# Sixteen units of attention and feed-forward on one core: the first unit's attention starts one unit earlier, and three smaller edits

## The chip, the cores and the metric

One core of one Trainium2 chip runs the whole program. The metric is the device time in microseconds (us). The kernel before takes 980.73 us, the median of three runs (980.03 to 981.28).

## The reference, cut to what matters

```python
x = x + _layernorm(attn(_layernorm(x)))      # x: 4 x 1024 x 512, float32
x = x + _layernorm(ffn(_layernorm(x)))

def attn(x):                                 # 16 heads of 32, chunks of 128 rows
    q, k, v = split(x @ w_qkv.T + b_qkv)     # 512 -> 3 * 512
    # per chunk and head, with S carried from chunk to chunk
    inter  = einsum(q * decay_q, S)
    scores = einsum(q, k) * dmask
    out    = inter + einsum(scores, v)
    S      = lam_c * S + einsum(k * decay_k, v)
    return out @ w_out.T + b_out

def ffn(x):                                  # weights rounded to float8_e4m3fn, then used as float32
    return ((silu(x @ gate_w * gate_s) * (x @ up_w * up_s)) @ down_w) * down_s   # 512 -> 1536 -> 512
```

## The kernel before, in words

The 4096 rows are 16 units of 256 rows (two tiles of 128). Float32 numbers are carried as a float16 half and a float16 rest (hi and lo), so one product is two or three float16 matmuls. The program is written as five queues by hand, one for each engine: TensorE (PE) multiplies, ScalarE (ACT) makes the hi halves and the normalised rows, GpSimd (POOL) makes the lo halves, the roots of the variances and the residual sums, VectorE (DVE) empties PSUM, and SyncE (SP) issues nearly all DMAs. Every engine runs its queue strictly in order, and semaphores hold it where it needs another one.

There are four stages. **Preparation** loads the QKV weights in four pieces (`w_in`), takes their largest value (DVE L1280, one reduction for each piece), spreads it over the partitions with a matmul (`spread_w_max`), makes a power of two of it, and splits the weights into hi (ACT L490, `w_hi`) and lo (DVE L1304, `w_lo`), for k, v and q in this order. ACT turns to `x_normalise(1)` and `x_hi(1)` between the second and the third `w_hi`. Unit 0's q doesn't wait for the split: `project_first` computes it from the float32 weights, output by output, once all four pieces are there. **Ahead**: for k = 0 to 13 (`LEAD` is 14) `ahead(k)` projects q, k and v of unit k and spills them to DRAM; DVE also rounds the feed-forward weights there. **Mixed slots**: `first_slot` runs the attention of unit 0 between the projections of unit 14, `second_slot` runs the attention of unit 1, the output projection of unit 0 and the projection of unit 15. **Slots** 2 to 17: slot s runs the attention of unit s, the output projection of unit s-1 and the feed-forward of unit s-2.

The steps by their names: `project_qk(n, i)` is 24 matmuls of 256 columns, i = 0, 1 for q and 2, 3 for k; `project_v(n, t)` is 12 matmuls of 512 columns; `scores(s, c, half)` is 8 small matmuls for chunk c, in two groups of heads, into the banks `b_s`; `masked` (DVE L1430) takes them out of PSUM, `probs_hi` (ACT L569) and `probs_lo` (POOL L1118) split them, and `attend(s, c)` multiplies them with v when all four groups of the chunk are split. `carry_and_state(s, c)` is the recurrent part; its sum is split by `state_hi` (ACT L581) and `state_lo` (DVE L1460), and the next chunk's carry waits for it. `k_lo(n, i)` (DVE L1409, L1416) empties a bank of k, and `project_v(n, t)` waits for it where v uses the same banks. `project(u, t)` is the output projection; behind it come `y_moments` (DVE), `inverse_std_of` (POOL L1050, L1053, L1057), `y_normalise` (ACT), `residual` (POOL L1128), `x1_moments`, again a root, `x1_hi` (ACT), `x1_lo` (POOL L1132) and a transposing DMA (`turn_x1`), and then `gate_up(u, 0)` (PE L919).

A bank is shared between stages: units below 14 put v into `b_s`, so that `scores(0, 0, 0)` waits for `v_sum` of unit 13. In the **last slot** only the feed-forward of unit 15 is left: `gate_up` six times, `down` for tile 0 and tile 1 (PE L937), and for each tile the scale (DVE L1532), the moments, the root on POOL, `y2_normalise` on ACT (L493), the sum with x (POOL L1142, `final`) and the store by SP (L400).

## Time and profile before

| | us |
|---|---|
| median of three runs | 980.73 |
| the profiled execution, its own time | 980.54 |
| its span, first to last instruction | 978.7 |
| TensorE busy | 949.6 |
| VectorE, GpSimd, ScalarE busy | 696.8, 691.3, 510.6 |
| granted TensorE clock, mean | 0.997 |

Times in the profile are counted from the start of the span; between the span and the run's own time lie 1.84 us. A line name such as L919 is the line of the source. A row of the timeline has the start, the length, the engine and line, what is written and read, how many instructions are merged, and in brackets how long the engine sat idle before and what released it. Matmuls overlap, so that a row's length is a little more than the distance to the next.

### The profile page before, as it was taken

The page shows a single profiled execution, that of the slowest core. Times are in us where ns is not written, and L with a number is a line of the kernel's source. Part 1 is how long each engine was busy: PE and PEld are TensorE (multiplying, and loading weights), DVE is VectorE, ACT ScalarE, POOL GpSimd, SP SyncE. Part 2 cuts the span into 40 slices and gives each one's busy share as a digit, 9 for nine tenths or more (in the row PEclk, how much of TensorE's full clock was granted, in tenths as well). Part 3 has the DMA queues.
Part 4 walks back from the last instruction along what each step waited for, and adds up shares of the span by engine and source line. Part 5 has one row for each costly group of instructions (what it writes and reads, how often), then busy time and mean ns, then how long its engine had stood idle before and what let it go on. Part 6 is the DMA issues. An engine that isn't in the chain of part 4 may idle for free.

```text
span 978.7 us, 21882 instructions
## 1 busy us (share of the span) xinstructions
PE 949.6 (97%) x8412; PEld 700.8 (72%) x8412; DVE 696.8 (71%) x1357; ACT 510.6 (52%) x987; POOL 691.3 (71%) x839
## 2 busy tenths in 40 slices
PE   8999999999888999999999999999999999999996
PEld 7687777777666776867778776767767676776764
DVE  6999998985887775767567576766757676675422
ACT  5666555565655464636355463635546363544522
POOL 3799998887776585948567584856758495775633
PEclk9999999999999999999999999999999999999998
DMA  9798899989976673846658284665838475512100
GB/s 320 232 309 245 244 261 314 281 260 301 244 204 144 138 195 66 183 108 142 157 103 190 55 199 97 152 146 115 180 59 199 94 161 121 139 44 44 44 23 22
DMA packets 199354, 159.87 MB, mean 163 GB/s; under 512 B 141649, under 2 KB 141777, under 8 KB 199121
## 3 DMA queue, kind: packets, MB, share of 16 engines
q1 hardware_dynamic: 198384, 157.86, 65.3%
q8 instruction: 66, 1.08, 0.5%
q10 hardware_dynamic: 864, 0.61, 0.2%
q14 instruction: 40, 0.32, 0.1%
HBM read 82.93 MB, written 41.94 MB: 128 GB/s over the span
## 4 chain that ended last, share of the span: by engine, by line
PE 44%; DVE 18%; POOL 16%; issue 10%; DMA 4%; SPq 3%; ACT 3%; POOLq 0%; DVEq 0%; ACTq 0%
PE bank L919 18%; PE bank L937 17%; PE att L896 5%; DVE stats L1386 3%; POOL rstd L1053 3%; POOL att_pool L1118 3%; DMA dram_qk<-qk_hl 2%; POOL vv L1103 2%; DVE state_hl L1460 2%; POOL qk_hl L1083 2%; SPq L297 2%; DVE w_pool L1523 2%; POOL xr L1128 1%; POOL rstd L1050 1%; DVE state L1449 1%
## 5 line engine op out<-in xcount | busy, mean ns | idle before, releaser
L919 PE MATMUL bank<-f_pool,up_q 128*128 128x256 f16 x1536 | 183.7, 273 | 4.2 <-DVE w_pool L1523 2.8
L919 PE MATMUL bank<-f_pool,gate_q 128*128 128x256 f16 x1536 | 183.6, 273 | 4.1 <-ACT w_pool L617 3.9
L937 PE MATMUL bank<-down_q,w_pool 128*128 128x512 f16 x768 | 168.3, 379 | 0.0
L919 PEld LDWEIGHTS bank<-f_pool,up_q 128*128 128x128 f16 x1536 | 148.1, 98 | 26.8 <-DVE w_pool L1523 8.5
L919 PEld LDWEIGHTS bank<-f_pool,gate_q 128*128 128x128 f16 x1536 | 146.3, 98 | 26.9 <-ACT w_pool L617 6.5
L1118 POOL TENSOR_TENSOR att_pool<-p,att_pool 128x512 f16<-128x512 f32 x128 | 145.7, 1159 | 24.5 <-ACT att_pool L569 24.5
L1523 DVE SCALAR_TENSOR_TENSOR w_pool<-bank,us_t,w_pool 128x256 f32<-128x256 f32 x192 | 84.1, 480 | 109.9 <-ACT w_pool L617 54.7
L1050 POOL TENSOR_TENSOR rstd<-mv,eps_t 128x1 f32<-128x1 f32 (+1 forms) x113 | 32.4, 287 | 182.0 <-DVE mv L1392 181.8
L937 PEld LDWEIGHTS bank<-down_q,w_pool 128*128 128x128 f16 x768 | 74.1, 98 | 86.9
L1136 POOL TENSOR_TENSOR w_pool<-w_pool 128x512 f16<-128x512 f32 x96 | 111.2, 1164 | 29.3 <-ACT w_pool L623 29.2
L569 ACT CAST att_pool<-p 128x512 f16<-128x512 f32 x128 | 75.6, 619 | 53.7 <-DVE p L1430 53.0
L493 ACT ACTIVATE w_pool<-w_pool,rstd 128x512 f32<-128x512 f32 x32 | 26.0, 812 | 146.1 <-POOL rstd L1057 146.1
L1430 DVE TENSOR_TENSOR p<-bank,mask 128x512 f32<-128x512 f32 x128 | 83.2, 682 | 8.0 <-POOL att_pool L1118 5.3
L617 ACT ACTIVATE w_pool<-bank,gs_t 128x256 f32<-128x256 f32 x192 | 80.1, 467 | 11.8 <-PE bank L919 10.2
L896 PE MATMUL att<-wout_hl,o_t 128*128 128x512 f16 x360 | 80.1, 379 | 0.0
L623 ACT CAST w_pool<-w_pool 128x512 f16<-128x512 f32 x96 | 59.2, 617 | 37.1 <-DVE w_pool L1523 35.9
L1053 POOL TENSOR_TENSOR rstd<-rstd,eps_t 128x1 f32<-128x1 f32 (+1 forms) x113 | 70.7, 626 | 8.8
L1532 DVE TENSOR_TENSOR w_pool<-bank,ds_t 128x512 f32<-128x512 f32 x32 | 22.1, 692 | 76.2 <-PE bank L937 76.2
L896 PEld LDWEIGHTS att<-wout_hl,o_t 128*128 128x128 f16 x360 | 35.2, 98 | 39.3
L1449 DVE TENSOR_TENSOR state<-bank,state_d 32x128 f32<-32x128 f32 x112 | 32.0, 286 | 30.4 <-issue 29.3
L1142 POOL TENSOR_TENSOR w_pool<-xr,w_pool 128x512 f32<-128x512 f32 x32 | 40.7, 1271 | 17.7 <-ACT w_pool L493 17.7
L1460 DVE SCALAR_TENSOR_TENSOR state_hl<-state,state_hl 32x128 f16<-32x128 f32 x112 | 48.1, 430 | 6.0 <-ACT state_hl L581 4.9
(147 smaller groups left out, 1824.4 us busy)
## 6 DMA issues: line engine op xcount, KB each, us to landing
dram_qk<-qk_hl SPq DMA_DIRECT2D x64, 256.0 KB, 4.6
att_pool<-dram_qk SPq DMA_DIRECT2D x64, 256.0 KB, 6.0
f_pool<-dram_qk SPq DMA_DIRECT2D x64, 256.0 KB, 6.0
xr<-in_x SPq DMA_DIRECT2D x31, 512.0 KB, 4.6
dram_kd<-kd_hl SPq DMA_DIRECT2D x32, 256.0 KB, 2.8
dram_v<-vv SPq DMA_DIRECT2D x32, 256.0 KB, 4.4
qn_pool<-dram_qk SPq DMA_DIRECT2D x32, 256.0 KB, 9.1
out_x<-w_pool SPq DMA_DIRECT2D x32, 256.0 KB, 2.1
```

The lines of the kernel that those rows point to most:

```text
L569: nc.scalar.copy(pr_hl[:, 0, heads(g)], by_head(p32[:, g % 2])).then_inc(p_hi_d, 1)
L617: ins = nc.scalar.activation(sil[:, j], b_gate[:, j * TOK:(j + 1) * TOK], ACT.Silu, scale=gs_t[:, 2 * i + j:2 * i + j + 1])
L623: nc.scalar.copy(h_hl[:, 0, 2 * i:2 * i + 2].rearrange("p k t -> p (k t)"), h32[:, i % 2]).then_inc(h_hi_d, 1)
L896: ins = nc.tensor.matmul(b_y[t], o_mov(u)[:, a, k, t * P:(t + 1) * P], wout_hl[:, b, k], start=(k == 0 and n == 0), stop=(k == KT - 1 and ...
L919: ins = nc.tensor.matmul(b[:, j * TOK:(j + 1) * TOK], w[:, k, o * P:(o + 1) * P], x1_hl[:, v % 2, part, k], start=(k == 0 and part == 0), ...
L937: ins = nc.tensor.matmul((b_gate, b_up)[t][:, :], h_hl[:, part, k, t * P:(t + 1) * P], down_q[:, k], start=(k == 0 and part == 0), stop=(k ...
L1053: nc.gpsimd.tensor_tensor(rstd[:, ln, 0, cols], rstd[:, ln, 2, cols], eps_t[:, 1, cols], ALU.pow).then_inc(pow_d[ln], 1)
L1118: nc.gpsimd.tensor_tensor(pr_hl[:, 1, heads(g)], by_head(p32[:, g % 2]), pr_hl[:, 0, heads(g)], ALU.subtract).then_inc(p_lo_d, 1)
L1136: nc.gpsimd.tensor_tensor(h_hl[:, 1, 2 * i:2 * i + 2].rearrange("p k t -> p (k t)"), h32[:, i % 2], h_hl[:, 0, 2 * i:2 * i + 2].rearrange( ...
L1430: nc.vector.tensor_tensor(by_head(p32[:, g % 2]), by_head(b_s[g % 2][:, :]), mask[:, heads(g)], ALU.mult).then_inc(p_d, 1)
L1460: ins = nc.vector.scalar_tensor_tensor(out=state_hl[r, 1, :, r], in0=state[r], scalar=2.0 ** -STATE_SHIFT, in1=state_hl[r, 0, :, r], op0=A ...
L1523: ins = nc.vector.scalar_tensor_tensor(out=h32[:, i % 2, j * TOK:(j + 1) * TOK], in0=b_up[:, j * TOK:(j + 1) * TOK], scalar=us_t[:, 2 * i ...
```

## The change

There are four edits.

1. The attention of unit 0 begins in `ahead(13)`, which is now `last_ahead`: `scores(0, 0, 0)`, `scores(0, 0, 1)` and `carry_and_state(0, 0)` lie between the projections of unit 13. For this v of unit 13 goes to `b_gate` and `b_up` instead of `b_s`. The steps of the first and second slot move up by half a slot on all five queues, and `scores(1, 0, 0)` closes the first slot. In slot 2, PE does `carry_and_state(2, 0)` behind `gate_up(0, 0)` instead of before it.
2. Unit 0's q is computed by weight piece: `project_first(k)` runs the four outputs for piece k as soon as that piece has landed, into four banks. The spreading matmul stands in the middle of piece 2. On DVE, `moments_x(1)` moves from before the largest value's steps to behind them, and so stands directly before the first `w_lo`.
3. In the last slot ACT does `y2_normalise(14, 0)` behind the first silu of unit 15 instead of before it.
4. The last tile is computed in two halves of 256 columns. DVE subtracts the mean itself and multiplies and adds by halves when POOL has the root, and ACT and SP each store one half.

```diff
+            spill_v(LEAD - 1)
             load_xr(0)
-            spill_v(LEAD - 1)
             spill_q(LEAD)
+            turn_o_tile(0, 0)
             sp.wait_ge(score_mm, 8)
             load_unit(2, 0)
             load_unit(2, 1)
-            turn_o_tile(0, 0)
             spill_k(LEAD)
             sp.wait_ge(state_mm, 2)
             load_unit(2, 3)
+            spill_kd(LEAD)
             turn_o_tile(0, 1)
-
-            spill_kd(LEAD)
             spill_v(LEAD)
...
+            def last_ahead():
+                k = LEAD - 1
+                v_hi(k - 1)
+                q_hi(k, 0)
+                q_hi(k, 1)
+                k_hi(k, 2)
+                x_normalise(k + 2)
+                probs_hi(0, 0, 0)
+                k_hi(k, 3)
+                x_hi(k + 2)
+                kd_hi_half(k, 0)
+                probs_hi(0, 0, 1)
+                kd_hi_half(k, 1)
+                state_hi(0, 0)
...
             def first_slot():
-                probs_hi(0, 0, 0)
                 v_hi(LEAD - 1)
                 q_hi(LEAD, 0)
-                probs_hi(0, 0, 1)
-                state_hi(0, 0)
                 q_hi(LEAD, 1)
+                probs_hi(0, 1, 0)
                 k_hi(LEAD, 2)
-                probs_hi(0, 1, 0)
+                o_hi_tile(0, 0)
+                probs_hi(0, 1, 1)
+                k_hi(LEAD, 3)
                 kd_hi_half(LEAD, 0)
-                k_hi(LEAD, 3)
-                probs_hi(0, 1, 1)
-                o_hi_tile(0, 0)
+                state_hi(0, 1)
+                v_hi_tile(LEAD, 0)
                 kd_hi_half(LEAD, 1)
-                v_hi_tile(LEAD, 0)
-                state_hi(0, 1)
                 v_hi_tile(LEAD, 1)

             def second_slot():
                 n = LEAD + 1
+                o_hi_tile(0, 1)
                 q_hi(n, 0)
-                o_hi_tile(0, 1)
+                probs_hi(1, 0, 0)
                 q_hi(n, 1)
-                probs_hi(1, 0, 0)
                 state_hi(1, 0)
-                y_normalise(0, 0)
                 probs_hi(1, 0, 1)
                 k_hi(n, 2)
+                y_normalise(0, 0)
                 y_normalise(0, 1)
+                probs_hi(1, 1, 0)
                 k_hi(n, 3)
                 x1_hi(0, 0)
-                probs_hi(1, 1, 0)
                 x1_hi(0, 1)
                 probs_hi(1, 1, 1)
                 state_hi(1, 1)
...
+                if v == units - 1:
+                    y2_normalise(v - 1, 0)
...
+            def project_first(k):
+                pe.wait_ge(w_in[k], 16)
+                for o in range(KT):
+                    if k == 2 and o == 2:
+                        spread_w_max()
+                    ins = nc.tensor.matmul(q_first[o][:, 0:TOK], w_stage[:, k, o * P:(o + 1) * P], x_first[:, k],
+                                           start=(k == 0), stop=(k == KT - 1))
+                    if k == KT - 1 and o % 2:
+                        ins.then_inc(qk_mm, 1)
...
+            def down_by_halves(v):
+                pe.wait_ge(h_d, 6 * v + 6)
+                for h, b in enumerate((b_up, b_gate)):
+                    if h:
+                        pe.wait_ge(y2_d, 2 * v + 1)
+                    for k in range(IT):
+                        for part in range(2):
+                            ins = nc.tensor.matmul(b[:, cols(h)], h_hl[:, part, k, P:TOK], down_q[:, k, cols(h)],
+                                                   start=(k == 0 and part == 0), stop=(k == IT - 1 and part == 1))
+                    ins.then_inc(down_mm, 1)
...
+            def last_ahead():
+                k = LEAD - 1
+                for i in range(3):
+                    project_qk(k, i)
+                scores(0, 0, 0)
+                project_qk(k, 3)
+                scores(0, 0, 1)
+                project_v(k, 0)
+                carry_and_state(0, 0)
+                project_v(k, 1)
+
             def first_slot():
-                scores(0, 0, 0)
-                carry_and_state(0, 0)
                 project_qk(LEAD, 0)
-                scores(0, 0, 1)
                 project_qk(LEAD, 1)
-                project_qk(LEAD, 2)
                 attend(0, 0)
                 scores(0, 1, 0)
+                project_qk(LEAD, 2)
+                scores(0, 1, 1)
+                carry_and_state(0, 1)
                 project_qk(LEAD, 3)
-                scores(0, 1, 1)
                 project_v(LEAD, 0)
-                carry_and_state(0, 1)
                 project_v(LEAD, 1)
                 attend(0, 1)
+                scores(1, 0, 0)

             def second_slot():
                 n = LEAD + 1
-                scores(1, 0, 0)
                 project_qk(n, 0)
+                carry_and_state(1, 0)
+                scores(1, 0, 1)
                 project_qk(n, 1)
-                carry_and_state(1, 0)
                 project(0, 0)
-                scores(1, 0, 1)
                 project(0, 1)
                 project_qk(n, 2)
-                project_qk(n, 3)
                 attend(1, 0)
                 scores(1, 1, 0)
+                project_qk(n, 3)
+                scores(1, 1, 1)
                 project_v(n, 0)
-                scores(1, 1, 1)
                 carry_and_state(1, 1)
                 project_v(n, 1)
                 attend(1, 1)
...
+                    if s > 2:
+                        carry_and_state(s, 0)
+                gate_up(v, 0)
+                if s == 2:
                     carry_and_state(s, 0)
-                gate_up(v, 0)
...
+            def last_ahead():
+                k = LEAD - 1
+                inverse_std_x(k + 2)
+                v_lo(k - 1)
+                state_decay(0, 0)
+                q_lo(k, 0)
+                q_lo(k, 1)
+                probs_lo(0, 0, 0)
+                x_lo(k + 2)
+                kd_lo_half(k, 0)
+                probs_lo(0, 0, 1)
+                kd_lo_half(k, 1)
...
                 q_lo(n, 1)
+                probs_lo(1, 0, 1)
                 inverse_std_of(LN_Y, 0, 0)
+                inverse_std_of(LN_Y, 0, 1)
                 residual(0, 0)
-                probs_lo_block(1, 0, 2)
-                inverse_std_of(LN_Y, 0, 1)
-                probs_lo_block(1, 0, 3)
                 residual(0, 1)
+                state_decay(1, 1)
+                probs_lo(1, 1, 0)
                 inverse_std_of(LN_X1, 0, 0)
-                state_decay(1, 1)
                 inverse_std_of(LN_X1, 0, 1)
                 x1_lo(0, 0)
-                probs_lo(1, 1, 0)
+                probs_lo(1, 1, 1)
                 x1_lo(0, 1)
...
-                moments_x(1)
                 dve.wait_ge(w_max_all, 1)
-                link(nc.vector.tensor_reduce(col(6), b_gate[:, 0:P], AX.X, ALU.max))
+                link(nc.vector.tensor_reduce(col(6), b_y[0][:, 0:P], AX.X, ALU.max))
                 power_of_two(col(9), col(6), 2.0 ** -30, 2.0 ** 35)
                 link(nc.vector.tensor_scalar(col(10), col(9), 2.0 ** -5, None, ALU.mult))
                 nc.vector.reciprocal(col(11), col(10)).then_inc(w_scale_d, 1)
                 dve.wait_ge(w_scale_d, 1)
                 link(nc.vector.tensor_scalar(bqk[:, :], bqk[:, :], col(11), None, ALU.mult))
+                moments_x(1)
...
+            def last_part(h):
+                dve.wait_ge(down_mm, 2 * units + h)
+                nc.vector.tensor_tensor(y2[:, 1, cols(h)], (b_up, b_gate)[h][:, cols(h)], ds_t[:, cols(h)], ALU.mult).then_inc(y2_d, 1)
+                dve.wait_ge(y2_d, 2 * units + h)
+                nc.vector.bn_stats(stats[:, LN_Y, h], y2[:, 1, cols(h)]).then_inc(bn_d[LN_Y2], 1)
+
+            def last_tile_out():
+                dve.wait_ge(bn_d[LN_Y2], 2 * units + 1)
+                dve.wait_ge(rs_d[LN_Y2], 2 * units - 2)
+                nc.vector.bn_aggr(mv[:, LN_Y2, 1], stats[:, LN_Y]).then_inc(mv_d[LN_Y2], 1)
+                dve.wait_ge(mv_d[LN_Y2], 2 * units)
+                nc.vector.tensor_scalar(y2[:, 1], y2[:, 1], mv[:, LN_Y2, 1, 0:1], None, ALU.subtract).then_inc(centred_d, 1)
+                dve.wait_ge(centred_d, 1)
+                dve.wait_ge(pow_d[LN_Y2], 2 * units)
+                for h in range(2):
+                    nc.vector.scalar_tensor_tensor(out=y2[:, 1, cols(h)], in0=y2[:, 1, cols(h)],
+                                                   scalar=rstd[:, LN_Y2, 0, 1:2],
+                                                   in1=xr[:, (units - 1) % 3, 1, cols(h)], op0=ALU.mult, op1=ALU.add
+                                                   ).then_inc(last_d, 1)
...
+            def last_ahead():
+                k = LEAD - 1
+                moments_x(k + 2)
+                scale_h()
+                k_lo(k, 2)
+                dve.wait_ge(tab_in, 16 * N_TAB)
+                dve.wait_ge(*x_landed(units - 2))
+                masked(0, 0, 0)
+                k_lo(k, 3)
+                masked(0, 0, 1)
+                v_sum(k, 0)
+                carry_and_state(0, 0)
+                v_sum(k, 1)

             def first_slot():
-                masked(0, 0, 0)
-                carry_and_state(0, 0)
-                masked(0, 0, 1)
                 state_lo(0, 0)
-                k_lo(LEAD, 2)
                 masked(0, 1, 0)
                 out_sum(0, 0)
-                k_lo(LEAD, 3)
-                masked(0, 1, 1)
+                k_lo(LEAD, 2)
                 o_max(0, 0)
                 scale_o(0, slice(0, 1), 1)
-                v_sum(LEAD, 0)
+                masked(0, 1, 1)
                 o_lo_tile(0, 0)
                 carry_and_state(0, 1)
+                k_lo(LEAD, 3)
+                v_sum(LEAD, 0)
+                state_lo(0, 1)
                 v_sum(LEAD, 1)
                 out_sum(0, 1)
                 o_max(0, 1)
                 scale_o(0, slice(1, T), T)
-                state_lo(0, 1)
+                masked(1, 0, 0)
                 o_lo_tile(0, 1)
-                masked(1, 0, 0)

             def second_slot():
                 n = LEAD + 1
                 carry_and_state(1, 0)
+                masked(1, 0, 1)
                 y_moments(0, 0)
-                masked(1, 0, 1)
                 state_lo(1, 0)
                 y_moments(0, 1)
+                k_lo(n, 2)
                 x1_moments(0, 0)
-                k_lo(n, 2)
                 x1_moments(0, 1)
-                k_lo(n, 3)
                 masked(1, 1, 0)
                 out_sum(1, 0)
+                k_lo(n, 3)
                 masked(1, 1, 1)
```

## Rows read from the trace of the kernel before

**Rows 1.** Part 1 of the page: busy time, share of the span, instructions.

```profile
PE 949.6 (97%) x8412; PEld 700.8 (72%) x8412; DVE 696.8 (71%) x1357; ACT 510.6 (52%) x987; POOL 691.3 (71%) x839
```

**Rows 2.** Stretches: start:end, length; busy PE, PEld, DVE, ACT, POOL; clock, DMA share, GB/s.

```profile
42.80:237.10 194.30, 194.26 (x1474) 143.95 (x1471) 177.22 (x261) 117.49 (x231) 181.33 (x158) 1.00 0.99 274
237.10:297.30 60.20, 51.71 (x573) 38.90 (x573) 49.87 (x103) 34.54 (x70) 43.70 (x51) 1.00 0.88 226
```

**Rows 3.** Timeline of PE in the preparation.

```profile
12.54 1.97 PE L785 MATMUL bank<-f_pool,att_pool 128*128 128x256 f32 x8 [1.96 <-DMA att_pool<-in_w_qkv_t]
...
25.77 5.35 PE L826 MATMUL bank<-w_pool,o_t 128*128 128x512 f16 x24 [0.25 <-DVE w_pool L1304]
...
40.12 2.79 PE L811 MATMUL att<-xr,w_pool 128*128 128x256 f16 x24 [1.14 <-DVE qk_hl L1416]
```

**Rows 4.** Timeline of DVE in the preparation.

```profile
14.29 0.68 DVE L1386 BATCH_NORM_STATS2 stats<-xr 128x6 f32<-128x512 f32 x1
...
15.91 0.26 DVE L1286 TENSOR_REDUCE small<-bank 128x1 f32<-128x128 f32 x1
...
18.22 2.48 DVE L1304 SCALAR_TENSOR_TENSOR w_pool<-att_pool,small,w_pool 128x1024 f16<-128x1024 f32 x2 [1.02 <-ACT w_pool L490]
22.68 5.42 DVE L1304 SCALAR_TENSOR_TENSOR w_pool<-att_pool,small,w_pool 128x1024 f16<-128x1024 f32 x4 [1.98 <-ACT w_pool L490]
```

**Rows 5.** Timeline of ACT in the preparation.

```profile
16.96 2.19 ACT L490 ACTIVATE w_pool<-att_pool,small 128x1024 f16<-128x1024 f32 x2 [6.93 <-DVE small L1289]
19.06 1.51 ACT L493 ACTIVATE xr<-xr,rstd 128x512 f32<-128x512 f32 x2
```

**Rows 6.** Timeline of POOL: the roots of unit 1, and a root at 106 us.

```profile
16.07 0.20 POOL L1050 TENSOR_TENSOR rstd<-mv,eps_t 128x2 f32<-128x2 f32 x1 [5.28 <-DVE mv L1392]
...
17.16 0.51 POOL L1057 TENSOR_SCALAR rstd<-mv,rstd 128x1 f32<-128x1 f32 x2
...
105.84 2.24 POOL L1050 TENSOR_TENSOR rstd<-mv,eps_t 128x2 f32<-128x2 f32 x1
```

**Rows 7.** Timeline of DVE at 105 us.

```profile
104.78 3.24 DVE L1346 SCALAR_TENSOR_TENSOR wout_hl<-qn_pool,small,wout_hl 128x2048 f16<-128x2048 f32 x1
```

**Rows 8.** Timeline of PE in the mixed slots.

```profile
221.34 5.40 PE L811 MATMUL bank<-xr,w_pool 128*128 128x256 f16 x48
...
297.34 1.91 PE L919 MATMUL bank<-f_pool,gate_q 128*128 128x256 f16 x16
```

**Rows 9.** Timeline of DVE in the mixed slots.

```profile
230.88 0.88 DVE L1409 SCALAR_TENSOR_TENSOR kd<-att,bqk,decay_k 128x256 f32<-128x256 f32 x2 [2.08 <-issue]
...
247.03 4.27 DVE L1460 SCALAR_TENSOR_TENSOR state_hl<-state,state_hl 32x128 f16<-32x128 f32 x4 [3.55 <-ACT state_hl L581]
```

**Rows 10.** Groups of instructions, 237.0 to 297.3 us: line, shapes, count, busy us, mean ns.

```profile
L1118 POOL TENSOR_TENSOR att_pool<-p,att_pool 128x512 f16<-128x512 f32 x16 | 18.2, 1159 | 10.9 <-ACT att_pool L569 10.9
...
L1430 DVE TENSOR_TENSOR p<-bank,mask 128x512 f32<-128x512 f32 x16 | 10.3, 684 | 2.5 <-PE bank L839 1.9 <-POOL att_pool L1118 0.4
...
L1409 DVE SCALAR_TENSOR_TENSOR kd<-bank,bqk,decay_k 128x256 f32<-128x256 f32 x8 | 3.5, 477 | 0.7 <-ACT qk_hl L540 0.6
```

**Rows 11.** Timeline of SP: transposed loads of kd from DRAM.

```profile
264.42 4.94 SPq L373 DMA_TRANSPOSE kt<-dram_kd  x1
...
312.26 11.62 SPq L373 DMA_TRANSPOSE f_pool<-dram_kd  x1
```

**Rows 12.** Timeline of PE and then ACT in the last slot.

```profile
943.06 1.92 PE L919 MATMUL bank<-f_pool,gate_q 128*128 128x256 f16 x16 [0.78 <-ACT w_pool L617]
...
941.47 0.81 ACT L493 ACTIVATE w_pool<-w_pool,rstd 128x512 f32<-128x512 f32 x1 [11.64 <-POOL rstd L1057]
```

**Rows 13.** Timeline of DVE and then POOL behind the last matmul.

```profile
971.10 0.69 DVE L1532 TENSOR_TENSOR w_pool<-bank,ds_t 128x512 f32<-128x512 f32 x1 [3.54 <-PE bank L937]
...
974.93 1.26 POOL L1142 TENSOR_TENSOR w_pool<-xr,w_pool 128x512 f32<-128x512 f32 x1 [0.93 <-ACT w_pool L493]
```

**Rows 14.** Part 6 of the page: DMA issues, size, us to landing.

```profile
out_x<-w_pool SPq DMA_DIRECT2D x32, 256.0 KB, 2.1
```

More of the change, by code:

```diff
@@ L482, in _ @@
             store(units - 1, 0)
-            store(units - 1, 1)
-            for t in range(T):
-                sp.wait_ge(stored[t], 16 * units)
+            sp.wait_ge(last_d, 2)
+            sp.dma_start(last_tile[:, cols(1)], y2[:, 1, cols(1)]).then_inc(stored[1], 16)
+            sp.wait_ge(stored[0], 16 * units)
+            sp.wait_ge(stored[1], 16 * (units + 1))
         @block.scalar
@@ L1168, in ahead @@
                                             ).then_inc(root_d, 1)
-            for k in range(LEAD):
+            for k in range(LEAD - 1):
                 ahead(k)
@@ L1249, in slot @@
                 final(v, 0)
+            last_ahead()
             first_slot()
```

82 lines of the change are left out of this document (42 added, 40 removed).

## The prediction

> **What bounds the kernel.** I read the page's busy times first, then stretches, then the timelines of the stretches in which TensorE (PE) isn't full. PE is busy 949.6 of 978.7 us, the next engine 696.8 [rows 1]. The change takes no matmul away, so it can win at most PE's idle 29 us, and only where they lie. From 42.8 to 237.1 us PE is busy 194.26 of 194.30 us: whatever delays PE before 42.8 comes through whole, and nothing given there is lost later. From 237.1 to 297.3, the two mixed slots, PE idles 60.20 - 51.71 = 8.5 us [rows 2]. Before 12.54 it idles 1.96, at 25.77 0.25 and at 40.12 1.14 us [rows 3]. In the last slot it idles 0.78 [rows 12], and behind its last matmul at 971.05 the chain of the last tile takes the rest.
>
> **Edit 2, the preparation: forecast 3.0 us slower.** Eight float32 records took 1.97 us [rows 3], so a piece of q costs 1.9. From 12.54 - 1.96 = 10.6 us on PE does pieces 0 and 1 and half of piece 2, until about 15.2, then the spread; DVE can read it from about 15.5, where L1286 began at 15.91 [rows 4]. That is 0.4 earlier, and `w_hi` starts at 16.5 instead of 16.96 [rows 5]. PE's own time is not the gain: L826 at 25.77 waited for DVE's fourth `w_lo`, and L811 at 40.12 for DVE too [rows 3], so DVE's chain sets PE's place.
> That chain loses. `moments_x(1)`, 15.91 - 14.29 = 1.6 us [rows 4], was beside PE's spread; now it runs from 16.8 to 18.5, behind the scaling of the biases, and its result reaches POOL at 18.55 instead of 16.07. POOL's root takes 17.16 + 0.51 - 16.07 = 1.6 us when nothing holds it [rows 6]: then ACT begins `x_normalise(1)` at 20.15 instead of 19.06 [rows 5], and the third `w_hi` behind it, the third and fourth `w_lo`, L826 and everything on DVE up to 40.12 move by 1.1. But two `w_lo`, 2.48 us for two [rows 4], now start at the moment POOL does, and both read two tensors of SBUF. At 105.84 the same L1050 took 2.24 us, from inside DVE's L1346 (104.78 to 108.02), a form with two such inputs, until just after its end; free, it took 0.20 [rows 6, 7]. Held like this, POOL's first step ends with the first `w_lo` at 19.7, its power at 20.95 + 0.6, the two products 0.6 later: ACT starts at 22.1, 3.0 late. Bounds 1.1 and 3.0; I take 3.0, because the row that resembles it is the held one. `w_lo` 1 itself is only 0.3 later, within PE's old idle. Queued behind the waiting ACT are the other four `w_hi` and `q_hi(0)`, all late by the same 3.0.
> The Trainium skill, "SBUF — State Buffer", section "SBUF: two separate sides", calls the port pair of VectorE and GpSimd an exclusive lock: a VectorE instruction with two SBUF inputs or in a two-port mode keeps it to its end, and the other "fully blocks". This speaks against the edit. By that rule the delay is 3.0, without it 1.1; the rows at 105 us agree with it.
>
> **Edit 1, the mixed slots: forecast 0.4 us faster.** I walk PE from 221.34 [rows 8], the start of `project_qk(13, 0)`, as if edit 2 weren't there. 24 matmuls of 256 columns take 2.62 (48 of them 5.24), `project_v` 2.59, `scores` 0.44 a call, carry and state 1.34, `attend` 0.86. Old stalls go: for v of unit 13, for the state's lo half (L1460 took 4.27 at 247.03 beside POOL [rows 9] and now has five us of room), for `masked(0, 1, 0)` behind it. New ones come:
> - `scores(0, 0, 1)`: PE is there at 232.3; `k_lo(13, 2)` starts at 230.88 [rows 9], takes 1.66 (four L1409/L1416 of 0.48, overlapping), then `masked` 0.68 [rows 10]: 233.2, and its second group. 1.3 us.
> - `project_v(14, 1)` waits for `k_lo(14, 3)`. From the end of `project_qk(14, 2)` DVE needs k_hi 1.0, k_lo 1.7, maximum and scale 1.3, masked 1.2, o_lo 0.8, carry and state 1.8, k_lo 1.7: 9.5. PE has 0.44 + 1.34 + 2.62 + 2.59 = 7.0. 2.4 us.
> - `scores(1, 1, 1)`: ACT's `y_normalise(0, 0)` now stands behind `k_hi(15, 2)`, that is behind PE; then come two residuals, two x1 moments, `masked(1, 1, 0)`: 6.0 against PE's 3.9. 2.1 us and 0.4 for the second group.
> - `attend(1, 1)` waits for POOL: two `probs_lo` 2.3, two roots 2.3, one `x1_lo` beside two `x1_hi`, two more `probs_lo` of 1.16 [rows 10]: 9.2 against PE's 6.6. 2.6 us.
> - `gate_up(0, 0)`: `x1_lo(0, 1)` stands last on POOL, then a transpose with 3.1 to land: 2.9 us.
> Together 11.7 us, against 8.5 in [rows 2]. The walk has PE at `gate_up(0, 0)` at 297.35, before it was 297.34 [rows 8], with 1.34 of `carry_and_state(2, 0)` still to do. These fill PE's waits in slot 2, whose DVE and POOL steps come 0.3 to 0.6 earlier, since `state_lo(1, 1)` no longer delays `out_sum(1, 1)`. Net -0.4. Each of the three middle stalls may be off by 0.7, and the walk by 3 in all: bounds +3 and -4. The moved DMAs (`turn_o_tile(0, 0)` ahead of unit 2's loads, `spill_kd(14)` ahead of `turn_o_tile(0, 1)`) are hidden: the first has 14 us, the second 1.8 us of room.
>
> **Edit 3: 0.9 us faster.** L919 at 943.06 waited 0.78 for a silu that stood behind ACT's L493, which waited for POOL until 941.47 [rows 12]. Now the silu runs at 940.6 and PE goes on at 942.1. POOL's `final(14, 0)` isn't later. Nothing else is late next.
>
> **Edit 4: 1.85 us faster.** Before, from the last matmul's end (971.05) to `final`'s end (974.93 + 1.26 = 976.19) are 5.1 us [rows 13]. After: scale, moments of 256 columns 0.85 instead of 1.4, joined 0.2, together 1.1; root without its third step 0.9, plus 0.3 if DVE's centring (it reads and writes SBUF at double rate) holds POOL's first step; two products by halves 0.9. That is 3.2 to 3.3; the last store is issued 1.85 earlier and lands in 2.1 as before [rows 14]. 48 matmuls of 256 columns cost 5.24 instead of 5.19: +0.05. Bounds 1.5 and 2.2.
>
> **Sum.** +3.0 - 0.4 - 0.9 - 1.85 = -0.15. The profiled execution was 980.54 (978.7 span, 1.84 around it): 980.4; the median of the runs is 0.19 above it: 980.6.
>
> **Rivals.** *POOL isn't held.* ACT goes on at 20.15, edit 2 costs 1.1: 978.7. For it: the small steps are 0.2 us and might slip in between two `w_lo`. Against it: [rows 6, 7].
> *The mixed slots fill.* If the stalls at `project_v(14, 1)` and `scores(1, 1, 1)` don't come, 4 us are won: 976.6. For it: 8.5 us of idle are there. Against: PE has 7.0 us to hide 9.5 of DVE.
> *SP's transposed load (slower).* `load_unit(2, 3)` and now `spill_kd(14)` stand ahead of `turn_o_tile(0, 1)`, and `project(0, 1)` waits for that. The load held SP's queue 4.94 us once and 11.62 another time [rows 11]. From 6.7 on it costs; at 11.6 PE waits 4.9 at `project(0, 1)`, and all of unit 0's x1 chain with it: 985.5. Against it: the same load stood there before and took 4.94.
> *The halves bring nothing*, since the first store on ACT's queue lands late: 982.4.
>
> **Chances.** The forecast 0.52, POOL not held 0.18, filled slots 0.14, SP 0.10, halves 0.06. A measurement tells about 0.2%, 2 us, from no change. Faster: the second rival, most of the first, and a little of the forecast: 0.31. Slower: SP's case, half of the halves', the forecast with the walk's upper bound: 0.19. Same: 0.50. The range 977.2 to 983.4 holds the forecast, its walk's error and the first rival, and leaves out most of the second and SP's case.
>
> **What would show it.** Right: POOL's L1050 of unit 1 lasting over 1 us beside L1304; the third `w_hi` at about 24.5; L811 with its wait at 43 instead of 40.12; PE waiting about 2.4 for `k_lo(14, 3)` and for POOL before `attend(1, 1)`; no wait before the second gate of the last slot; 3.3 us from the last matmul to the last product. Wrong: the fourth `w_lo` ending before 27, or PE idle under 7 us over the mixed slots.

## The result and the profile after

The changed kernel takes **988.93 us**, the median of six runs (986.86 to 992.15); the kernel before took 981.0 beside it. The ratio is 1.0077, with an interval of 1.0057 to 1.0097. The forecast was 980.6 with a range of 977.2 to 983.4: the kernel is slower by 8 us, and the time lies outside.

The profiled execution took 988.03, its span is 986.2, 7.5 more than before. Starts of the same step in the two timelines of PE say where that arose. `project_v(1, 0)` begins at 45.62 instead of 42.75 (+2.87), `project_qk(13, 0)` at 223.86 instead of 221.34 (+2.52), `down` of unit 0 at 340.86 instead of 330.14 (+10.72), and the first `gate_up` of unit 15 at 949.33 instead of 938.63 (+10.70). So the preparation cost 2.5 to 2.9, the mixed slots and slot 2 cost 8.20, and the last slot gave 3.2 back.

Three stretches of the changed kernel, from `project_qk(13, 0)` to `down` of unit 0 (columns as in [rows 2]):

```profile
223.86:239.60 15.74, 14.53 (x129) 11.61 (x128) 9.51 (x30) 10.01 (x20) 13.88 (x17) 1.00 1.09 283
239.60:307.28 67.68, 55.24 (x543) 38.82 (x542) 49.16 (x101) 33.30 (x69) 44.60 (x51) 0.92 0.83 201
307.28:340.86 33.58, 33.58 (x352) 27.75 (x353) 25.59 (x56) 20.21 (x41) 24.38 (x32) 0.95 0.78 181
```

The same work in the kernel before, cut at the same steps:

```profile
221.34:237.10 15.76, 15.76 (x121) 11.65 (x119) 9.01 (x28) 9.32 (x19) 14.44 (x17) 1.00 1.08 287
237.10:297.34 60.24, 51.75 (x574) 38.94 (x574) 49.87 (x104) 34.54 (x70) 43.74 (x51) 1.00 0.88 225
297.34:330.14 32.80, 31.37 (x332) 25.35 (x331) 25.39 (x54) 20.20 (x41) 24.24 (x31) 1.00 0.86 185
```

Add the columns. Before, 108.80 us with PE busy 98.88: idle 9.92. After, 117.00 us with PE busy 103.36: idle 13.64. The loss of 8.20 is 3.72 of idle and **4.48 of busy time for the same matmuls**. The clock (third column from the end) says why: 0.92 and 0.95 instead of 1.00. This divides the time by what PE did in it; it is not yet the price of the clock, since a slow row can fill a wait that would have come anyway.

PE's rows with a wait, and the slow rows, in the changed kernel's timeline (they answer to [rows 8]):

```profile
235.96 0.40 PE L867 MATMUL bank<-att_pool 128*128 128x128 f16 x4 [1.01 <-DVE p L1494]
261.13 2.76 PE L854 MATMUL bank<-w_pool,o_t 128*128 128x512 f16 x12 [2.15 <-DVE qk_hl L1480]
279.43 5.13 PE L924 MATMUL att<-wout_hl,f_pool 128*128 128x512 f16 x12 [4.61 <-DMA f_pool<-hl]
292.93 0.40 PE L867 MATMUL bank<-f_pool 128*128 128x128 f16 x4 [1.80 <-DVE p L1494]
293.76 4.44 PE L854 MATMUL bank<-w_pool,xr 128*128 128x512 f16 x12
303.00 0.19 PE L910 MATMUL att<-f_pool,att_pool 128*128 128x64 f16 x1 [0.88 <-issue]
307.28 2.80 PE L947 MATMUL bank<-f_pool,gate_q 128*128 128x256 f16 x16 [2.80 <-DMA f_pool<-hl]
309.87 2.74 PE L947 MATMUL bank<-f_pool,up_q 128*128 128x256 f16 x16
```

Five of these six waits had been walked. The third had not: `project(0, 1)` waits 4.61 us for the turned o tile. Twelve matmuls of 512 columns take 2.75 at full clock; here they take 5.13 and 4.44. Over the first of them the granted clock was 0.52 (third column from the end), nearly all of it at the lower of the two levels, 1.2 GHz. The four slow rows together are 5.8 longer than at full clock (2.38 + 1.69 + 0.89 + 0.83); the other rows of the three stretches show 1.3 less busy time than before, which was not traced further.

```profile
279.40:284.50 5.10, 5.07 (x13) 1.89 (x14) 0.00 (x0) 0.00 (x0) 0.00 (x0) 0.52 0.94 265
```

What SP did at that time answers to [rows 11]:

```profile
257.71 1.24 SPq L315 DMA_TRANSPOSE f_pool<-hl  x1
259.06 3.90 SPq L366 DMA_DIRECT2D att_pool<-dram_qk  x8
263.00 0.91 SPq L339 DMA_DIRECT2D dram_qk<-qk_hl  x2
264.01 10.71 SPq L382 DMA_TRANSPOSE kt<-dram_kd  x1
274.76 1.05 SPq L345 DMA_DIRECT2D dram_kd<-kd_hl  x2
275.86 1.30 SPq L315 DMA_TRANSPOSE f_pool<-hl  x1
```

`load_kt(2)` held the queue 10.71 us, not 4.94. Two rows above it stand unit 2's eight loads from `dram_qk`, 2 MB in all: the "stack loads". In the kernel before they were issued well ahead of the load of kd, which began at 264.42 there:

```profile
254.68 3.64 SPq L357 DMA_DIRECT2D att_pool<-dram_qk  x8
```

The last row is `turn_o_tile(0, 1)`, issued 5.9 us later than in the kernel before.

The preparation in the changed kernel, rows of POOL, DVE, ACT and PE that answer to [rows 3 to 6]:

```profile
18.09 1.14 POOL L1096 TENSOR_TENSOR rstd<-mv,eps_t 128x2 f32<-128x2 f32 x1 [7.51 <-DVE mv L1456]
19.31 1.63 POOL L1099 TENSOR_TENSOR rstd<-rstd,eps_t 128x2 f32<-128x2 f32 x1
...
17.92 2.45 DVE L1368 SCALAR_TENSOR_TENSOR w_pool<-att_pool,small,w_pool 128x1024 f16<-128x1024 f32 x2
...
21.58 1.52 ACT L502 ACTIVATE xr<-xr,rstd 128x512 f32<-128x512 f32 x2 [3.36 <-POOL rstd L1103]
24.03 2.19 ACT L499 ACTIVATE w_pool<-att_pool,small 128x1024 f16<-128x1024 f32 x2
...
28.29 7.01 PE L854 MATMUL bank<-w_pool,o_t 128*128 128x512 f16 x24 [3.10 <-DVE w_pool L1368]
```

And the end of the last tile, which answers to [rows 13]: DVE's last scale, centring and product, and POOL's root.

```profile
980.91 0.42 DVE L1601 TENSOR_TENSOR w_pool<-bank,ds_t 128x256 f32<-128x256 f32 x1 [1.64 <-PE bank L978]
982.08 0.51 DVE L1610 TENSOR_SCALAR w_pool<-w_pool,mv 128x512 f32<-128x512 f32 x1
983.10 0.88 DVE L1614 SCALAR_TENSOR_TENSOR w_pool<-w_pool,rstd,xr 128x256 f32<-128x256 f32 x2 [0.51 <-POOL rstd L1190]
...
982.12 0.19 POOL L1187 TENSOR_TENSOR rstd<-mv,eps_t 128x1 f32<-128x1 f32 x1 [1.35 <-DVE mv L1608]
```

### The profile page after: what moved, and what is told of

It is laid out like the page before. It is cut to its first block, busy times and chain, and to the rows that moved or that the text cites. A ratio compares the mean times of both kernels' runs of the same rounds, so it can differ in the third digit from the quotient of the medians.

```text
span 986.2 us, 21932 instructions
## 1 busy us (share of the span) xinstructions
PE 954.9 (97%) x8436; PEld 706.0 (72%) x8436; DVE 698.5 (71%) x1362; ACT 509.4 (52%) x986; POOL 692.1 (70%) x837
## 4 chain that ended last, share of the span: by engine, by line
PE 51%; POOL 16%; DVE 14%; issue 9%; SPq 3%; DMA 3%; ACT 2%; POOLq 0%; DVEq 0%; ACTq 0%
PE bank L947 20%; PE bank L965 16%; PE att L924 6%; POOL rstd L1099 3%; POOL att_pool L1164 3%; DVE stats L1450 2%; POOL qk_hl L1129 2%; POOL vv L1149 2%; PE att L910 2%; POOL rstd L1096 2%; DMA dram_qk<-qk_hl 1%; POOL xr L1174 1%; SPq L306 1%; DVE w_pool L1587 1%; POOL rstd L1103 1%
## 5 line engine op out<-in xcount | busy, mean ns | idle before, releaser
L965 PE MATMUL bank<-down_q,w_pool 128*128 128x512 f16 x744 | 163.1, 379 | 0.0
L965 PEld LDWEIGHTS bank<-down_q,w_pool 128*128 128x128 f16 x744 | 71.7, 98 | 84.1
```

The source lines that it names most:

```text
L965: ins = nc.tensor.matmul((b_gate, b_up)[t][:, :], h_hl[:, part, k, t * P:(t + 1) * P], down_q[:, k], start=(k == 0 and part == 0), stop=(k ...
```

## The experiments

Each kernel ran beside the kernel before, whose median was 981.58, 981.06, 981.07 and 980.98 in the four groups. A ratio is always to the kernel before; intervals stand in brackets. "Dummy products" are matmuls whose result nobody reads.

### Four first experiments

**a_sp**: the changed kernel with the suspected load behind the turned tile.

```diff
             spill_k(LEAD)
-            sp.wait_ge(state_mm, 2)
-            load_unit(2, 3)
             spill_kd(LEAD)
             turn_o_tile(0, 1)
+            sp.wait_ge(state_mm, 2)
+            load_unit(2, 3)
```

> The changed kernel with one thing moved in SP's queue: the transposed load of unit 2's kd goes behind turn_o_tile(0, 1) instead of standing before it. Theory (SP's load is the loss): PE's wait of 4.6 us at project(0, 1) goes, and with it the half-clock stretches behind it (project(0, 1) 5.13 instead of 2.75 us, project_v(15, 0) 4.44 instead of 2.75, gate_up(0, 0) 5.5 instead of 3.7): 7 to 8 us less than the changed kernel, about 981.5. Rival (the order on PE, DVE, ACT and POOL is the loss, and the load only fills a wait that would be there anyway): less than 2 us, about 987.

Measured 984.46, 1.0026 [1.0010, 1.0042]: 4.5 us under the changed kernel, between the theory (981.5) and its rival (987). But `project(0, 1)` still waited, 2.13 us, though its tile had been issued at 269.30:

```profile
269.30 2.25 SPq L315 DMA_TRANSPOSE f_pool<-hl  x1
271.65 4.72 SPq L382 DMA_TRANSPOSE kt<-dram_kd  x1
...
276.76 4.36 PE L924 MATMUL att<-wout_hl,f_pool 128*128 128x512 f16 x12 [2.13 <-DMA f_pool<-hl]
```

It landed 7.4 us after its issue; in the changed kernel that took 3.6. So the load had a part in it, and something else too. The tile landed 14.0 us after the last stack load had been issued (262.7).

**a_mx**: the changed kernel with `moments_x(1)` back in its old place on DVE.

```diff
+                moments_x(1)
                 dve.wait_ge(w_max_all, 1)
...
-                moments_x(1)
                 for n, part in enumerate((1, 2, 0)):
```

> The changed kernel with moments_x(1) on DVE back before the steps of the largest value; q is still computed by weight piece. Theory (the shared port holds POOL's root): POOL's first step of unit 1 falls from 1.14 to 0.2 us, ACT starts x_normalise(1) at about 18.2 instead of 21.58, PE's waits of 3.1 us before project_v(0, 0) go, and PE reaches unit 3 about 2.9 us earlier: 986 against 988.9. Rival (q by piece itself costs time, by PE's lower clock or the matmul for the largest value): PE is still over 1.5 us late at unit 3.

Measured 985.16, 1.0035 [1.0020, 1.0049]. POOL's first root step took 0.19 again, and the fourth `w_lo` no longer made PE wait:

```profile
16.54 0.19 POOL L1096 TENSOR_TENSOR rstd<-mv,eps_t 128x2 f32<-128x2 f32 x1 [5.74 <-DVE mv L1456]
16.81 0.71 POOL L1099 TENSOR_TENSOR rstd<-rstd,eps_t 128x2 f32<-128x2 f32 x1
```

Two rows of the same run show what the half clock costs where a wait follows. `project_v(15, 0)` ran at full clock here, and `attend(1, 1)` then waited 2.55; in the changed kernel they were 4.44 and 0.88, which is the same sum:

```profile
291.80 2.75 PE L854 MATMUL bank<-w_pool,xr 128*128 128x512 f16 x12
...
301.03 0.19 PE L910 MATMUL att<-f_pool,att_pool 128*128 128x64 f16 x1 [2.55 <-issue]
```

**c_all** is both edits together.

> Both of the former edits together. Theory (two separate losses): their gains add, 978 to 979, about 2 to 3 us less than the kernel before, since the last slot's 3 us are then all that is left. Rival (one hides the other): at most the larger gain, 981.5.

Measured 982.05, 1.0011 [0.9999, 1.0024], 2.4 under a_sp, and 3 us over what its theory had (978 to 979): the two gains, 4.5 and 3.8, add to 6.9 only. With a_mx, the moved moments cost 2.4 to 3.8 us. `project_v(14, 1)` and `project_v(15, 0)` took 4.39 and 4.44 here.

**b_tail** is the kernel before with edits 3 and 4 alone (the last slot and the halves).

> The kernel before with the two edits of the last slot alone (y2_normalise(14, 0) behind the silu; the last tile by halves). Theory: 0.9 from PE's wait before the second gate and 2.2 from the chain behind the last matmul, 977.9 against 981.0. Rival (the halves only looked cheap because PE came later): under 1 us, 980.2.

Measured 977.29, 0.9961 [0.9946, 0.9976]. A second time, in the last group, it gave 978.24, 0.9966 [0.9948, 0.9984]. These two edits are worth 2.7 to 4.3 us, and c_all, which has them, is 4.8 above the first figure: edit 1 still loses about 4 to 5 us with the load out of the way. In b_tail's own profiled execution a stall that the kernel before has, too (1.79 + 0.20), was followed by half clock: the 12 matmuls of `project_v(14, 0)` at 254.58 took 4.44 at a granted clock of 0.61. In the kernel before and in b_tail's second time the same matmuls took 2.75.

### Edit 1 by itself, the load, the clock, q by piece

**e_mix**: edit 1 alone, with the old start and the old last slot.

> Edit 1 alone on the kernel before (the old start, the old last slot). The changed kernel was 8.0 us over the kernel before: start 2.5 to 2.9, mixed slots 8.2, last slot -3.2. Theory (the mixed slots carry it all, whatever the start does): 8.2 over the kernel before, 989 us, PE waits at project(0, 1) about 4.6 us for the turned o tile and runs its first matmuls behind three of its waits at half clock. Rival (the mixed slots only go wrong because the start shifted them against the DMAs): 3 over, 984 us. The prediction's own price for this edit was 0.4 us faster.

Measured 989.19, 1.0073 [1.0052, 1.0094]: 7 to 8 us, as its theory had it, and not the 3 of its rival. The start has no part in it. In its profiled execution, which was the fastest of its runs (986.14), the stretches sum to 114.33 us with PE busy 102.67: 1.7 more idle than before and 3.8 more busy. There `project(0, 1)` waited 2.94 and then ran at full speed (2.76), and `project_v(14, 1)`, `project_v(15, 0)` and the first gate and up ran slow (4.45, 4.44, 2.77, 2.76).

**a_o0**: the changed kernel with `turn_o_tile(0, 0)` back behind unit 2's stack loads.

```diff
-            turn_o_tile(0, 0)
             sp.wait_ge(score_mm, 8)
             load_unit(2, 0)
             load_unit(2, 1)
+            turn_o_tile(0, 0)
             spill_k(LEAD)
```

> The changed kernel with turn_o_tile(0, 0) back behind unit 2's eight stack loads on SP. Theory (load_kt(2) holds SP's queue until some 11.5 us after the last stack load was issued): the stack loads end at 259.5 instead of 263.0, load_kt ends near 271 instead of 274.8 and lasts 9 us instead of 10.7, project(0, 1) waits 1 us instead of 4.6: 3.5 to 4.5 us under the changed kernel, 985 us. Rival (load_kt lasts 4.9 whenever a turned tile is issued between it and the stack loads, as it was in the kernel before): load_kt ends at 267, project(0, 1) does not wait, 983.5. Second rival (its length has nothing to do with the stack loads): 10.7 us as now, no gain.

Measured 987.09, 1.0057 [1.0040, 1.0074]. The load lasted 8.48 and ended at 273.66, 13 us after the last stack load instead of the 11.5 expected:

```profile
255.70 4.88 SPq L366 DMA_DIRECT2D att_pool<-dram_qk  x8
260.63 3.30 SPq L315 DMA_TRANSPOSE f_pool<-hl  x1
265.18 8.48 SPq L382 DMA_TRANSPOSE kt<-dram_kd  x1
...
278.37 4.45 PE L924 MATMUL att<-wout_hl,f_pool 128*128 128x512 f16 x12 [1.96 <-DMA f_pool<-hl]
```

Both rivals fall (no end at 267, and not 10.7), the direction is the theory's; the gain was 1.8, half of what was expected. The first turned tile, now issued directly behind the stack loads (260.63), held the queue 3.30 only, but landed 10.7 us after its issue; ahead of them it landed 4.6 after it in the changed kernel.

**a_warm**: the changed kernel with dummy products in two of PE's waits.

```diff
+            def keep_busy(count, out):
+                for n in range(count):
+                    nc.tensor.matmul(out, wqkv_hi[:, 0, 0:P], wqkv_hi[:, 0, 0:2 * P], start=True, stop=True)
...
+                if (u, t) == (0, 1):
+                    keep_busy(38, b_y[1][:, 0:2 * P])
                 pe.wait_ge(o_turned[t], 16 * (u + 1))
...
+                    if v == 0:
+                        pe.wait_ge(v_d, 2 * units)
+                        keep_busy(22, b_gate[:, 0:2 * P])
                     pe.wait_ge(x1_turned, 32 * (v + 1))
```

> The changed kernel with TensorE products whose result nobody reads put in ahead of two of its long waits: 38 of 256 columns ahead of the wait for project(0, 1) (4.1 us) and 22 ahead of that for gate_up(0, 0) (2.4 us). The waits stay as long. Theory (the granted clock falls because PE stands still, and the work behind the wait then runs at half speed): project(0, 1) takes 2.75 instead of 5.13 us and the first gate 1.91 instead of 2.80: 3 to 4 us under the changed kernel, 985.5. Rival (the clock falls for another reason, or it costs nothing since PE would wait for the same DVE and POOL steps later): no change, 989.

Measured 986.44, 1.0046 [1.0029, 1.0063]: 2.5 under the changed kernel, less than expected. The clock did what the theory says. Behind the dummies the same matmuls ran at full speed:

```profile
276.37 4.31 PE L918 MATMUL att<-w_pool 128*128 128x256 f16 x38
281.89 2.76 PE L930 MATMUL att<-wout_hl,f_pool 128*128 128x512 f16 x12 [1.22 <-DMA f_pool<-hl]
...
308.27 1.91 PE L956 MATMUL bank<-f_pool,gate_q 128*128 128x256 f16 x16
```

In this execution the turned tile landed 5.4 us after its issue instead of 3.6, which took back 1.8 us; why, no run shows.

**b_tail_q**: edits 3 and 4 with q by weight piece, the moments in their old place.

> The kernel before with edits 3 and 4 (977.3 us measured) and q by weight piece, but with the moments of x tile 1 left where they were. Theory (q by piece alone gives DVE its scale 0.4 us earlier, and all that hangs on DVE's chain with it, while the held root came from the moved moments): 0.4 under the kernel with edits 3 and 4 alone, 976.9. Rival (the first q finishes in another order and the scaled q of unit 0 and what turns behind it come later, as the wait of 3.4 us at the first k in the kernel with the moments moved back suggests): 0.5 to 1 over it, 978.

Measured 978.39, 0.9970 [0.9957, 0.9984]: level with edits 3 and 4 alone (977.29, 978.24). Finishing q by piece is worth nothing here. PE fills with it a time in which it then waits 3.17 for the turned x (`20.93`, L828), and DVE's chain sets the place of what follows.

### The load first, and the repairs

**a_kt**: the changed kernel with `load_kt(2)` ahead of everything else.

```diff
             spill_q(LEAD)
+            sp.wait_ge(state_mm, 2)
+            load_unit(2, 3)
             turn_o_tile(0, 0)
             sp.wait_ge(score_mm, 8)
             load_unit(2, 0)
             load_unit(2, 1)
             spill_k(LEAD)
-            sp.wait_ge(state_mm, 2)
-            load_unit(2, 3)
             spill_kd(LEAD)
```

> The changed kernel with load_kt(2) on SP ahead of turn_o_tile(0, 0) and of the eight stack loads, nothing else. Theory (a transposed load of kd holds SP's queue until what was put on the queue just ahead of it has gone, so it is short where no stack load stands ahead of it, and the wait at project(0, 1) is its work): load_kt lasts 3 to 5 us from 255.7, turn_o_tile(0, 1) goes at 269 to 270, project(0, 1) waits for nothing and is not behind a fall of the clock: 4.6 + 2.4 = 7 us under the changed kernel, 982. Rival (the load takes its 10.7 wherever it stands): turn_o_tile(0, 0) and the stack loads wait behind it, project(0, 0) waits 1 to 2 us instead, 984 to 986.

Measured 985.80, 1.0056 [1.0036, 1.0077]. Half of the theory held, and the other half fell:

```profile
256.23 4.56 SPq L382 DMA_TRANSPOSE kt<-dram_kd  x1
260.83 1.30 SPq L315 DMA_TRANSPOSE f_pool<-hl  x1
262.24 3.85 SPq L366 DMA_DIRECT2D att_pool<-dram_qk  x8
...
269.84 3.69 SPq L315 DMA_TRANSPOSE f_pool<-hl  x1
...
278.18 2.76 PE L924 MATMUL att<-wout_hl,f_pool 128*128 128x512 f16 x12 [3.00 <-DMA f_pool<-hl]
```

The load was short, 4.56, with no stack load ahead of it. Yet the turned tile, issued at 269.84, landed at 278.2, 12 us after the last stack load. **The load was only the first victim.** Each transposing DMA that stood shortly behind the eight stack loads landed or ended late: a_sp's and a_kt's tile, a_o0's first tile, the load itself.

**c_warm**: c_all with dummy products ahead of `project_v(14, 1)`, `project(0, 1)`, `scores(1, 1, 1)` and `gate_up(0, 0)` (17, 7, 14, 22).

> The kernel with both repairs (load_kt(2) behind turn_o_tile(0, 1); moments of x tile 1 left where they were; 982.05 us measured) with products that nobody reads put into four waits of TensorE: 17 of 256 columns ahead of project_v(14, 1), 7 ahead of project(0, 1), 14 ahead of scores(1, 1, 1), 22 ahead of gate_up(0, 0). Theory (of what the mixed slots lose, some 5 us is work at half clock behind waits: project_v(14, 1) 4.39, project_v(15, 0) 4.44, the first gate and up 3.23 and 2.32, which take 2.75, 2.75, 1.91 and 1.91 at full clock): 4 to 5 us less, 977.5. Rival (the half clock costs nothing, because PE would only wait longer for DVE and POOL): 982.

Measured 979.80, 0.9986 [0.9976, 0.9995]: 2.3 under c_all, half of what was expected. `project_v(14, 1)` and `project_v(15, 0)` took 2.76 and 2.75 again, but `attend(1, 1)` waited 2.56 instead of 0.86 for POOL: what the faster `project_v(15, 0)` gave, the wait took back.

**e_fix**: edits 1, 3 and 4 with the old start, the load first, and two steps of the walk's stalls put earlier.

```diff
                 o_lo_tile(0, 0)
-                carry_and_state(0, 1)
                 k_lo(LEAD, 3)
+                carry_and_state(0, 1)
...
-                k_hi(n, 2)
                 y_normalise(0, 0)
+                k_hi(n, 2)
```

> Edits 1, 3 and 4 with the old start, load_kt(2) first on SP, k_lo(14, 3) ahead of carry_and_state(0, 1) on DVE, and y_normalise(0, 0) ahead of k_hi(15, 2) on ACT. Theory (the walk's stalls of 2.15 at project_v(14, 1) and of 1.8 at scores(1, 1, 1) come from these two places in the order, each with 1.7 us of half clock behind it; edits 3 and 4 give 4): mixed slots 3 to 5 us shorter than with the load repaired alone, 974 to 976, which is under the kernel with edits 3 and 4 alone (977.3). Rival (each repaired stall comes back at the next place, since DVE and POOL are full there): 978 to 980.

Measured 984.28, 1.0030 [1.0015, 1.0045], a miss of 8 us and more, and above the rival's 978 to 980, too. The two stalls did shrink (2.15 to 1.18, 1.80 to 0.89). But PE came earlier to `project(0, 1)`, whose tile lay behind the stack loads as in a_kt, and waited 2.74 there, then 2.54 and 2.72 at the places behind it.

**e_fix_w**: the same with 22 dummies ahead of `gate_up(0, 0)`.

> The kernel above with 22 products that nobody reads (256 columns each) ahead of gate_up(0, 0)'s wait for the turned x1. Theory: the first gate and up run at full clock, 1.7 us less than the kernel above. Rival: no change.

Measured 980.95, 1.0004 [0.9987, 1.0021]: 3.3 less, where 1.7 was expected. The first gate and up of e_fix, 3.60 and 2.81 instead of 1.92 and 1.91, explain 2.6. Both kernels scatter more than the others (980.1 to 986.8 and 979.0 to 987.5): in e_fix_w's profiled execution, 984.12, `project(0, 1)` waited 4.79 instead of 2.74. The place of the turned tile differs between executions, so the 3.3 is not all the clock's.

### The stack loads behind the turned tile

**a_late**: the changed kernel with nothing altered but this.

```diff
             turn_o_tile(0, 0)
-            sp.wait_ge(score_mm, 8)
-            load_unit(2, 0)
-            load_unit(2, 1)
             spill_k(LEAD)
             sp.wait_ge(state_mm, 2)
             load_unit(2, 3)
             spill_kd(LEAD)
             turn_o_tile(0, 1)
+            sp.wait_ge(score_mm, 8)
+            load_unit(2, 0)
+            load_unit(2, 1)
```

> The changed kernel with unit 2's eight stack loads (2 MB) on SP behind turn_o_tile(0, 1); load_kt(2) stays ahead of it. Theory (transposing DMAs on SP's queue end only when the stack loads issued before them have drained, some 11 us after the last issue, 2 MB at about 200 GB/s; edit 1 brought the turned tile into that time): load_kt lasts about 4.6 us, turn_o_tile(0, 1) is issued at 269.5 to 270.5 and lands within 4 us, project(0, 1) waits at most 0.3 us and no half clock follows it: 5 to 7 us under the changed kernel, 982 to 984. Rival (the turned tile lands late for a reason of its own, the other traffic of that time): project(0, 1) still waits 3 us, 986.

Measured 983.46, 1.0026 [1.0014, 1.0038]: 5.5 under the changed kernel, inside what the theory said. The profiled execution, 985.44, is one of the slower; `project_v(13, 0)` and `project_v(14, 1)` ran slow in it (4.44, 4.08). The load took 1.89, and both tiles of `project(0)` ran in one row without a wait and at full clock:

```profile
264.52 1.89 SPq L382 DMA_TRANSPOSE kt<-dram_kd  x1
273.58 1.24 SPq L315 DMA_TRANSPOSE f_pool<-hl  x1
274.92 3.85 SPq L366 DMA_DIRECT2D att_pool<-dram_qk  x8
...
276.15 5.34 PE L924 MATMUL att<-wout_hl,f_pool 128*128 128x512 f16 x24
```

The DMA view shows the draining itself: bytes moved in 40 slices of 262 to 276 us, first of the changed kernel, then of a_late.

```profile
GB/s 181 205 222 211 205 187 187 205 222 228 187 187 187 205 240 211 187 205 187 205 205 205 211 205 222 205 228 182 240 381 404 315 293 45 23 23 142 291 288 290
```

```profile
GB/s 207 187 11 0 0 0 6 351 410 316 211 250 260 271 232 274 287 351 404 398 392 129 0 0 0 0 0 0 0 0 0 0 0 0 0 0 94 218 210 202
```

The stack loads move 2 MB at some 200 GB/s, which fills the DMA engines until 272.2. Only then does the load of kd run, at 300 to 400. In a_late nothing stands ahead of it, and from 269.8 the engines stand empty until the turned tile comes. Plain DMAs wait in the same way: the two spills of k that are issued directly behind the stack loads (263.0) landed 11.4 us after their issue in the changed kernel, and 2.4 us in a_late. They don't hold SP, which went on after 0.91; the load of kd does.

**f_late** is e_fix with SP's order of a_late (both turned tiles ahead of the stack loads, and `load_kt(2)` between the tiles); **f_late_w** has 8, 6 and 22 dummies ahead of `project_v(14, 1)`, `scores(1, 1, 1)` and `gate_up(0, 0)`.

> Edits 1, 3 and 4 with the old start, the stack loads behind turn_o_tile(0, 1), load_kt(2) ahead of both, k_lo(14, 3) ahead of carry_and_state(0, 1) and y_normalise(0, 0) ahead of k_hi(15, 2). Theory (with the turned tile in time, edit 1 costs only its stalls of 1.2, 0.9, 2.5 and 2.7 us, as large as those of the kernel before, and the half clock behind some of them): 978 to 980, 5 us under the same kernel with the loads ahead (984.3). Rival (all stalls of the mixed slots move together, as the rival for that kernel had it): 982 to 984.

> The kernel above with products that nobody reads (256 columns each) put into TensorE's waits: 8 ahead of project_v(14, 1), 6 ahead of scores(1, 1, 1), 22 ahead of gate_up(0, 0). Theory (the clock): 2 to 3 us less than the kernel above, 976.5. If so, edit 1 repaired is level with leaving it out (977.3). Rival: no change.

> The kernel before with edits 3 and 4 alone once more, beside the three above: 977.3 by all theories, which makes 3.8 us the worth of the last slot's edits.

Measured: f_late 978.68, 0.9977 [0.9965, 0.9989], 5.6 under e_fix. f_late_w 977.05, 0.9970 [0.9956, 0.9985]. b_tail2 978.24. The repaired edit 1 is level with leaving edit 1 out. Each beats the kernel before by 2 to 4 us and the changed kernel by 10 to 12. f_late_w has the lowest median, b_tail2 (0.9966 [0.9948, 0.9984]) the lowest ratio: the three can't be told apart, and neither can f_late_w's gain of 1.6 over f_late (0.7 by the ratios).

## Why the prediction was wrong, by its own steps

- **The step that failed** is the last sentence on edit 1: "the second has 1.8 us of room". The room was nearly right: with a hold of 10.71 PE waited 4.61, so the load costs from 6.1 us on, where the prediction had 6.7. What was wrong is the hold of `load_kt(2)` it was worked out with, 4.94 [rows 11], taken over from the kernel before. That row was short because the stack loads had been issued by 258.3, six us ahead of it. Edit 1 puts `turn_o_tile(0, 0)`, which waits until 257.7, ahead of them, and they end at 262.96, directly ahead of the load. The other row of the same group, 11.62 behind stack loads, was the one to use. Both rows say the same when read by their end: the load of 4.94 ended 11.0 us after the last stack load was issued, the load of 11.62 ended 13.1 after, and that of 10.71 in the changed kernel 11.8 after. The slower rival named the place and even the wait (4.9, measured 4.6), and gave it a chance of 0.10. Its price, 985.5, was low in part because it counted no clock. Taking the stack loads out of the way (a_late) won 5.5 of the 8.3 us by which the forecast missed.
- **A term that was missing**: the granted clock. The walk priced each stall at its length. Behind stalls, four rows of matmuls took 5.8 us more than at full clock, and busy time grew by 4.48. Not all of it is loss: the 1.69 at `project_v(15, 0)` came off the wait at `attend(1, 1)`. Dummy products in the waits brought 2.5 (a_warm against the changed kernel), 2.3 (c_warm against c_all) and 3.3 (e_fix_w against e_fix, with the doubt named there) back; the 1.6 of f_late_w against f_late is within the noise. So the clock is worth some 2 to 3 us here. In the rows of the kernel before the clock stays at 1.00 where it stalls, and nothing in them gave a price; b_tail shows that the same stall can be followed by half clock.
- **The walk was right** in what it walked. Its stalls of 1.3, 2.4, 2.1 + 0.4 and 2.9 came as 1.01 + 0.20, 2.15, 1.80 + 0.20 and 2.80. The 2.6 at `attend(1, 1)` came as 0.88 where `project_v(15, 0)` ran at half clock (the changed kernel, c_all, e_mix, a_o0, a_kt: 4.44 and 0.86 to 0.88), and as 2.55 where it didn't (a_sp, a_mx, a_late: 2.75 and 2.55). Idle grew by 3.72, the unforeseen wait is 4.61; without it, and with 2.55 at `attend(1, 1)`, idle grows by 0.8, against the forecast of -0.4 and its bounds of +3 and -4. That edit 1 would win anything is not borne out: with the late tile repaired (c_all) it still cost 4 to 5, and at best (f_late, f_late_w) it is level with leaving it out.
- **Edit 2 was right** in that the moved moments hold POOL's root, and nearly by size: 2.5 to 2.9 in the trace, 2.4 to 3.8 in the runs, forecast 3.0. POOL's step lasted 1.14 beside `w_lo` and its power 1.63; with the moments back 0.19 and 0.71. The Trainium skill's rule of the shared port pair ("SBUF — State Buffer", section "SBUF: two separate sides") spoke against the edit, and the trace agrees. The third `w_hi` came at 24.03, forecast 24.5. But PE's wait stood at 28.29, not at 43: PE lost 3.10 there, the 24 matmuls behind took 7.01 instead of 5.35 at a granted clock of 0.75, and the old wait at 40.12 was gone. That the size came out so near is in part luck: a longer wait at another place, and a half clock that the walk didn't have.
- **Edit 3 was right**: the second gate has no wait. **Edit 4 was right**: 3.1 us from the last matmul's end to the last product's, forecast 3.2 to 3.3. DVE's centring did not hold POOL (0.19 beside it). Both together: forecast 2.75, measured 3.2 in the trace, 2.7 to 4.3 in the runs.
- The sum was -0.15; by the trace it should have been 2.5 + 8.2 - 3.2 = 7.5.

## What to carry to other kernels

A duration taken from a row holds only with what stood ahead of it on the same queue: before an edit moves a transposing DMA or the bulk loads ahead of it, look at every row of that DMA and at when it ends, counted from the last of the loads. In the kernel before, 14 of the 16 loads of kd stand behind stack loads. They held the queue for 4.94 to 11.62 us, median 10.0, but all ended 10.4 to 13.1 us after the last stack load had been issued, the short one 11.0 after. So the trace of the kernel before already showed it. Where a schedule lets TensorE stall for about 2 us, give the stall a second price with the matmuls behind it at half clock, as a bound, and ask whether a later wait takes it up.
